# Expert weights in one transfer each, the last two bodies of an eight-image pipeline merged, and own weight sets and four banks for the last experts

## What is computed

```
x = x + deformable_conv(group_norm(x))             # F: 9 taps, gathered by learned offsets
x = x + top_ranks(sort(corr(group_norm(x))))       # S: every token's 1024 correlations sorted, 128 ranks kept
t = t + local_attention(layer_norm(t))             # C: windows 4, 16, 32
t = t + moe(layer_norm(t))                         # C: 8 experts 128 -> 128 -> 128, gelu, top 2 gates
t = t + state_space(layer_norm(t))                 # C: 8 heads, state 32
t = t + moe(layer_norm(t))                         # M: 8 experts, hidden 341, silu(h1) * h3, top 2 gates
```

## Time and profile before

| what | us |
|---|---|
| median of 3 runs | 5278.51 (5259.53 to 5298.2) |
| profiled execution | 5287.57 |
| its span, first to last instruction | 5285.8 |
| VectorE busy | 4563.2 (86%) |
| TensorE busy | 4040.3 (76%), mean granted clock 0.851 |
| ScalarE busy | 3051.8 (58%) |
| GpSimd busy | 927.3 (18%) |

### The profile page before, as it was taken

How to read it: one execution, slowest core, us unless ns; L and a number is a source line. 1 busy time by engine, 2 the same in 40 slices (tenths; PEclk the granted TensorE clock), 3 DMA queues, 4 the chain that set the end, 5 groups by cost and what they waited for, 6 DMA issues and landing times.

```text
span 5285.8 us, 59716 instructions
## 1 busy us (share of the span) xinstructions
PE 4040.3 (76%) x19026; PEld 2678.5 (51%) x19026; DVE 4563.2 (86%) x5779; ACT 3051.8 (58%) x7094; POOL 927.3 (18%) x580
## 2 busy tenths in 40 slices
PE   5665638988698868988698877988599876776487
PEld 4554325745366544755366444755357453443254
DVE  0298899999999999999999999999999999999721
ACT  4554226865487636866477646866377655653364
POOL 2253002600053002600044001610035000000000
PEclk8887568998799878998799888998799988886698
DMA  4232002310132012310032011310033000000011
GB/s 131 84 105 57 16 0 70 110 31 21 34 101 74 28 30 69 100 43 17 28 96 86 27 34 44 109 48 24 26 91 94 23 25 27 29 24 18 0 29 36
DMA packets 226078, 269.68 MB, mean 51 GB/s; under 512 B 26831, under 2 KB 188506, under 8 KB 225626
## 3 DMA queue, kind: packets, MB, share of 16 engines
q0 software_dynamic: 46080, 151.03, 9.8%
q1 hardware_dynamic: 179674, 114.65, 7.4%
HBM read 242.25 MB, written 23.34 MB: 50 GB/s over the span
## 4 chain that ended last, share of the span: by engine, by line
DVE 36%; PE 30%; issue 13%; ACT 8%; DMA 5%; POOL 4%; SPq 3%; DVEq 0%; POOLq 0%; ACTq 0%
PE bank L595 6%; POOL gath L733 4%; DVE srt_a L770 4%; DVE srt_b L770 3%; DMA gath<-quads,idx 3%; PE bank L1190 3%; DVE srt_a L813 2%; SPq L500 2%; DVE srt_b L813 2%; PE bank L1503 2%; PE bank L1507 2%; DVE srt_b L802 2%; DVE srt_a L802 2%; ACT diag L628 2%; DVE srt_a L768 2%
## 5 line engine op out<-in xcount | busy, mean ns | idle before, releaser
L733 POOL DMA_INDIRECT gath<-quads,idx x576 | 927.1, 1609 | 3137.6 <-DVE idx L704 2570.7
L595 PE MATMUL bank<-diag,gath 128*128 128x128 f32 x4608 | 619.0, 297 | 173.6 <-DMA gath<-quads,idx 173.6
L628 ACT ACTIVATE diag<-ident,w 128x128 f32<-128x128 f32 x2304 | 697.6, 391 | 12.8 <-DVE w L717 12.6
L595 PEld LDWEIGHTS bank<-diag,gath 128*128 128x128 f32 x4608 | 593.4, 211 | 205.1 <-DMA gath<-quads,idx 128.9
L1503 PE MATMUL bank<-mu_t,e2w 128*128 128x512 f32 (+1 forms) x768 | 453.2, 675 | 134.8 <-DMA e2w<-moe_w_t 117.9
L1487 PEld LDWEIGHTS bank<-e2w,act 128*128 128x128 f32 (+1 forms) x3072 | 423.9, 203 | 199.5 <-issue 175.7
L1507 PE MATMUL bank<-gated_u,e2w 128*128 128x512 f32 (+1 forms) x768 | 438.5, 655 | 31.9 <-ACT h_s L1561 31.9
L1487 PE MATMUL bank<-e2w,act 128*128 128x128 f32 (+1 forms) x3072 | 428.4, 286 | 18.9 <-DVE act L1591 18.9
L1591 DVE TENSOR_TENSOR act<-act,h_s 128x512 f32<-128x512 f32 (+1 forms) x384 | 262.6, 686 | 167.6 <-ACT h_s L1561 160.1
L1555 ACT ACTIVATE act<-bank 128x512 f32<-128x512 f32 (+1 forms) x384 | 228.7, 595 | 309.2 <-PE bank L1503 307.1
L811 DVE TENSOR_TENSOR srt_a<-srt_b 128x1920 f32<-128x1920 f32 (+5 forms) x176 | 381.0, 2165 | 3.7
(11 more groups left out here) (319 smaller groups left out, 7740.2 us busy)
## 6 DMA issues: line engine op xcount, KB each, us to landing
e2w<-moe_w_t SPq DMA_DIRECT2D x256, 170.5 KB
quads<-xn_tok SPq DMA_DIRECT2D x256, 64.0 KB
e1w<-L_ffn_w SPq DMA_DIRECT2D x256, 64.0 KB, 2.0
e2w<-moe_w_t SPq DMA_DIRECT2D x256, 64.0 KB
gath<-quads,idx POOLq DMA_INDIRECT x576
e2w<-moe_w_t SPq DMA_DIRECT2D x128, 42.5 KB
x_tok<-x SPq DMA_DIRECT2D x8, 512.0 KB, 4.0
out<-tm SPq DMA_DIRECT2D x16, 256.0 KB, 2.5
```

The source lines that it names most:

```text
L595: ins = T.matmul(FB[q % 2][:, k * P:(k + 1) * P], gath[:, g % 2, k, s * C:(s + 1) * C], diag[:, g % 2, 4 * k + s], start=(s == 0), stop=(s ...
L628: ins = SC.activation(diag[:, g % 2, n], ident[:], ACT.Copy, scale=w[:, n:n + 1])
L733: pool.indirect_dma_start(gath[:, g % 2, k], None, quads, bass.IndirectOffsetOnAxis(idx[:, TG * g + k:TG * g + k + 1], 0)).then_inc(sem["g ...
```

## The change

1. *Weights packed.* On the host w1, w3 and w2 of a second expert are laid side by side in one array of 128 rows by 1066 numbers (w2 padded with zeros from 341 to 384 rows), those of a first expert in 128 rows by 256. SP issues one transfer for each expert instead of five or two; the semaphore counts follow.
2. *Bodies 7 and 8 in one.* The late body now also holds C(7,1), M(7,0) and M(7,1); the drain body and its strings are gone. The order within a stream stays.
3. *Last second experts, M(7,1).* Each of the eight experts has its own place, three in `srt_a`, three in `srt_b`, two in `corr`, and its own semaphore; SP issues the eight loads once half 1 of image 7 is ranked. Its h1, h3 and gated inputs go round four banks (FB[0], FB[1], MB[0], MB[1]) instead of two.
4. *New strings* for the full and late bodies on TensorE, ScalarE, SP and VectorE. Those of fill and early are as they were.

```diff
-    SP_full=(
-        "CCCMMFFCCCCCCCCMMMFMMMCCCCMMMCMMMMMMM"
+    SP_full=(
+        "CCCMMFFCCCCMCCCCMMMMMMMMFCCCCMCMMMMMM"
...
-    SP_late=(
-        "CCCMMMCCCMCCCCCMMMMMMMMMMMMMCCMCCC"
+    SP_late=(
+        "CCCMMMCCCMCCCCCMMMMMMMMMMMMMCCCMMMCCCCCMMMMCMCCCMCMMMMMMMMMM"
...
-                sp.dma_start(e1w[:, e % E1_SLOTS, 0], A["L2_ffn_w1"][e]).then_inc(sem["e1_in%d" % (e % E1_SLOTS)], 16)
-                sp.dma_start(e1w[:, e % E1_SLOTS, 1], A["L2_ffn_w2"][e]).then_inc(sem["e1_in%d" % (e % E1_SLOTS)], 16)
+                sp.dma_start(e1w[:, e % E1_SLOTS].rearrange("p a c -> p (a c)"), A["moe1_w_t"][e]).then_inc(sem["e1_in%d" % (e % E1_SLOTS)], 16)
...
+        def last_unit(i, h):
+            return isinstance(i, int) and i == IMGS - 1 and h == 1
+
+        def experts_w(i, h, e):
+            if not last_unit(i, h):
+                return e2w[:, e % 2]
+            size = 2 * HID + 3 * C
+            home = (srt_a, srt_b, corr)[e // 3][:].rearrange("p g n -> p (g n)")
+            return home[:, e % 3 * size:(e % 3 + 1) * size]
+
+        def wide_banks(i, h):
+            return (FB[0], FB[1], MB[0], MB[1]) if last_unit(i, h) else (MB[0], MB[1])
+
         def sp_M(sp, i, h):
             for e in range(E8):
-                sp.wait_ge(sem["y2_ps"], unit("y2_ps", i, h, max(0, 3 * (e - 1))))
+                if last_unit(i, h):
+                    sp.wait_ge(sem["ranked"], unit("ranked", i, h))
+                else:
+                    sp.wait_ge(sem["y2_ps"], unit("y2_ps", i, h, max(0, 3 * (e - 1))))
                 settle(sp)
-                sp.dma_start(e2w[:, e % 2, 0:HID], A["moe2_w1_t"][e]).then_inc(sem["e2_in%d" % (e % 2)], 16)
-                sp.dma_start(e2w[:, e % 2, W3:W3 + HID], A["moe2_w3_t"][e]).then_inc(sem["e2_in%d" % (e % 2)], 16)
-                for k, m in enumerate(HTILES):
-                    sp.dma_start(e2w[0:m, e % 2, W2 + k * C:W2 + (k + 1) * C],
-                                 A["moe2_w2_t"][e, k * P:k * P + m]).then_inc(sem["e2_in%d" % (e % 2)], 16)
+                arrived = last_in[e] if last_unit(i, h) else sem["e2_in%d" % (e % 2)]
+                sp.dma_start(experts_w(i, h, e), A["moe2_w_t"][e]).then_inc(arrived, 16)
                 yield
...
+            X = wide_banks(i, h)
             pe.wait_ge(sem["m_utsb"], unit("m_utsb", i, h))
+            if last_unit(i, h):
+                pe.wait_ge(sem["corr_sb"], img("corr_sb", i))
...
-                    if r >= 2:
-                        pe.wait_ge(sem["m_sb"], unit("m_sb", i, h, r - 1))
-                    T.matmul(MB[r % 2][0:m, :], e2w[:, e % 2, k * P:k * P + m], mu_t[:], start=True, stop=True).then_inc(sem["m_ps"], 1)
+                    if r >= len(X):
+                        pe.wait_ge(sem["m_sb"], unit("m_sb", i, h, r - len(X) + 1))
+                    T.matmul(X[r % len(X)][0:m, :], experts_w(i, h, e)[:, k * P:k * P + m], mu_t[:], start=True, stop=True).then_inc(sem["m_ps"], 1)
...
             body(IMGS - 1, False, True, True)
-            body(IMGS, False, False, True)
-
-        def second_of(make, eng, i, sort, second):
-
-            if second and sort:
+
+        def second_of(make, eng, i, first, sort, second):
+
+            if second and not first:
+                return both(make(eng, i - 1, 1), make(eng, i, 0), make(eng, i, 1))
+            if second:
                 return both(make(eng, i - 1, 1), make(eng, i, 0))
...
+        def experts_of(make, eng, i, first, second):
+
+            if not second:
+                return both()
+            if first:
+                return both(make(eng, i - 1, 0), make(eng, i - 1, 1))
+            return both(make(eng, i - 1, 0), make(eng, i - 1, 1), make(eng, i, 0), make(eng, i, 1))
```

The string of VectorE for the late body, before (its last 96 letters of 382; the drain body's 108 follow) and after (its last 202 of 490):

```diff
-        "SSSCSCSSCSSSSSSSSSSCSCSSCSSCCCCSSCSSCCSSSCSSSCCSSSCCSSSSSCCSSSSCSSCSSCSSSSSSSSSSSSSSSSSSSSSSSS"
+        "SSCSCSCSSSSSSSSSSCSCSSCSCCCCSCSSCSCSSSSCSSSCCSSSSCCSSSCCSSSSSCSSCSSCSMSMSSSMMMMMMSSSSMSMMSMSMSMS"
+        "SSSMSMSMSSSSMSMSSCMCCCMCCMMCCCCCCCCMCMCCMCCMMCMCCMCCMMCCCCCCCCCCCCCCCCCCCCMMMMMMMMMMMMMMMMMMMMMM"
+        "MMMMMMMMMM"
```

More of the change, by code:

```diff
@@ L120 @@
[L120 to L129, removed]
@@ L331, in build @@
         prep = ctx.enter_context(nc.semaphore("prep"))
+        last_in = [ctx.enter_context(nc.semaphore(f"last_in{e}")) for e in range(E8)]
         n_loads = [0]
@@ L1487, in y_part @@
                     ins = T.matmul(MB[2][:, t * P:(t + 1) * P], act2[0:m, n % ACT2_SLOTS, t * P:(t + 1) * P],
-                                   e2w[0:m, e % 2, W2 + k * C:W2 + (k + 1) * C], start=False,
+                                   experts_w(i, h, e)[0:m, W2 + k * C:W2 + (k + 1) * C], start=False,
                                    stop=(n == 3 * E8 - 1 and t == UT - 1))
@@ L1554, in act_M @@
                     act.wait_ge(sem["y2_ps"], unit("y2_ps", i, h, n - ACT2_SLOTS + 1))
-                SC.activation(act2[0:m, n % ACT2_SLOTS], MB[r % 2][0:m, :], ACT.Silu).then_inc(sem["m_sb"], 1)
+                SC.activation(act2[0:m, n % ACT2_SLOTS], X[r % len(X)][0:m, :], ACT.Silu).then_inc(sem["m_sb"], 1)
                 yield
@@ L1620, in run @@
             body(IMGS - 1, False, True, True)
-            body(IMGS, False, False, True)
-        def second_of(make, eng, i, sort, second):
-            if second and sort:
+        def second_of(make, eng, i, first, sort, second):
+            if second and not first:
+                return both(make(eng, i - 1, 1), make(eng, i, 0), make(eng, i, 1))
+            if second:
                 return both(make(eng, i - 1, 1), make(eng, i, 0))
-            if second:
-                return make(eng, i - 1, 1)
             if sort:
@@ L1631, in second_of @@
             return both()
-        def experts_of(make, eng, i, second):
-            return both(make(eng, i - 1, 0), make(eng, i - 1, 1)) if second else both()
+        def experts_of(make, eng, i, first, second):
[4 more added lines that the diff above has]
+            return both(make(eng, i - 1, 0), make(eng, i - 1, 1), make(eng, i, 0), make(eng, i, 1))
         block = ctx.enter_context(nc.Block())
@@ L1646, in body @@
                 weave(sp, "SP", kind_of(first, sort, second),
-                      dict(F=sp_first(sp, i, first, more), C=second_of(sp_C, sp, i, sort, second), M=experts_of(sp_M, sp, i, second)))
+                      dict(F=sp_first(sp, i, first, more), C=second_of(sp_C, sp, i, first, sort, second), M=experts_of(sp_M, sp, i, first, second)))
             def sp_first(sp, i, first, more):
@@ L1672, in body @@
                 weave(act, "ACT", kind_of(first, sort, second),
-                      dict(F=act_F(act, i, sort, first), C=second_of(act_C, act, i, sort, second), M=experts_of(act_M, act, i, second)))
+                      dict(F=act_F(act, i, sort, first), C=second_of(act_C, act, i, first, sort, second), M=experts_of(act_M, act, i, first, second)))
             run(act, body)
@@ L1684, in body @@
                            S=both(dve_S(dve, i, 0), dve_S(dve, i, 1)) if sort else both(),
-                           C=second_of(dve_C, dve, i, sort, second), M=experts_of(dve_M, dve, i, second)))
+                           C=second_of(dve_C, dve, i, first, sort, second), M=experts_of(dve_M, dve, i, first, second)))
             run(dve, body)
@@ L1705, in body @@
                 weave(pe, "PE", kind_of(first, sort, second),
-                      dict(F=pe_F(pe, i, sort, first), C=second_of(pe_C, pe, i, sort, second), M=experts_of(pe_M, pe, i, second)))
+                      dict(F=pe_F(pe, i, sort, first), C=second_of(pe_C, pe, i, first, sort, second), M=experts_of(pe_M, pe, i, first, second)))
             run(pe, body)
@@ L1743, in layouts @@
         w_out_t=t(a["L3_attn_W_out"].T.reshape(2, P, C).transpose(1, 0, 2)),
-        moe2_w1_t=t(a["L3_ffn_w1"].transpose(0, 2, 1)), moe2_w3_t=t(a["L3_ffn_w3"].transpose(0, 2, 1)),
-        moe2_w2_t=t(a["L3_ffn_w2"].transpose(0, 2, 1)),
+        moe1_w_t=t(np.concatenate([a["L2_ffn_w1"], a["L2_ffn_w2"]], 2)), moe2_w_t=t(packed),
   )
```

94 lines of the change are left out of this document (49 added, 45 removed).

## The result

The changed kernel takes 5344.4 us, median of 4 runs (5332.92 to 5358.25), against 5278.7 us of the kernel before in the same session. The ratio is 1.0124 with a 95% interval from 1.0101 to 1.0147: slower by 1.2%. The forecast was 5229 us, its range 5185 to 5272; both the sign and the range are missed.

A forecast was written before the change was run, and what follows sets the result against it. VectorE, busy 86% of the span, was taken to bound all but the end. Terms 13 - 21 - 35 - 6 = -49 gave 5238.6 us for the profiled execution, 5229 us from the median; range 5185 to 5272.

The forecast's parts named there:

- New strings for full bodies, 0: Six full bodies: VectorE's work is equal, so only waits change; 0 us, at most -174 if all waits went.
- Rival C: Full bodies: second experts' products not ready stop VectorE's sort, 1.2 us at each of 16, +118 to 5347 us; chance 0.12.
- M(7,0) ahead of the sort, +13: Late body: M(7,0) work moved before the sort's end makes the sort end 13 us later; bounds +10 and +22.
- C(7,1), -21: Last half image's attention, first experts and state space, with less M(7,0) beside them: 200.5 to 180 us; bounds -45 and +5.
- state-space term, 94 to 84: State-space part of C(7,1): 15 us of other work leaves the chain, 5 added for lower clock, 94 to 84 us.
- rival B: C(7,1) is bound by its own chain at the lower clock and stays at 200 us; 5250 us in all; chance 0.12.
- Own sets, -35: M(7,1): with own weight places six late experts take 8.46 us instead of 14.14; -35 us, bounds -28 and -40.
- Rival D: Moved loads or wide banks don't work, M(7,1) stays at 14.14 us an expert; 5263 us; chance 0.05.
- Four banks, 0: M(7,1): TensorE had no gap with two banks, so two more bring 0 us; bounds 0 and -4.
- one transfer per expert, -6: Weight loads: latency stays, only SP's issue time falls; 1 us per body, -6 us in six; bounds -20 to +10.
- Rival A: C(7,1) follows TensorE's work, -45 instead of -21, and full bodies lose 2 us of waits each; 5193 us; chance 0.24.

The follow-up runs named there:

- experiment 6: The kernel before with one packed transfer for each expert, first and second, and nothing else: 5272.91 us, ratio 0.9981.
- (7): Two runs from experiment 1: shared weight slots instead of own sets for M(7,1), 5274.15 us; two banks instead of four there, 5242.06 us.
- (8): experiment 1 with the last two bodies separate again, on the old late and drain strings; own weight sets and four banks stay: 5245.48 us, ratio 0.9929.
- experiment 1: The changed kernel with the full bodies' four strings of the kernel before, everything else of the change kept: 5247.52 us, ratio 0.9931.
- experiment 2: The kernel before with the four new strings for the full bodies and nothing else of the change: 5389.11 us, ratio 1.019.
- Experiment 4: The changed kernel with four first-expert weight slots instead of three and the fourth load ahead of the 32 transfers in SP's full string: 5281.0 us, ratio 0.9992.
- i1: experiment 1 with only the two banks MB[0] and MB[1] for M(7,1) instead of four, own weight sets kept: 5242.06 us, ratio 0.9933.

## Why the prediction was wrong

Measured parts, against the kernel before: packing -10 (experiment 6), own sets -27 (7), merge about 0 (8), banks 0 (7), full strings +97 (marks; experiment 1 gives 5344.4 - 5247.5 = 97 too, and experiment 2, in the kernel before, +107 by its marks). The sum is +60, and 5278.7 + 60 = 5339 us beside 5344.4 measured. Without the strings the parts are -37, where the forecast had -49, and experiment 1's 5247.5 us lies inside the stated range: the rest of the forecast held within 12 us.

**New strings for full bodies, 0: this step failed, and it alone turned the sign.** It measured +97 us. I had looked at how far second experts and first experts move against the sort, and not at F. With the new strings the group norm is done 8 us later and the 32 transfers start 10 us later, and SP holds the fourth load of the first experts behind them: VectorE's waits at the first experts grew by 75 us in six bodies. The strings also raised its waits at the second experts, by 28. Experiment 4 took the first cause away and left 49 us. The rows were there: the earlier trace rows was only the largest wait, while the 2.98 us of TensorE for that load, shown above, told that the load had no slack. "VectorE's work is equal, so only waits change" was right; that these would come out at zero had no row behind it. The reading of the strings was off too: VectorE's second experts stand earlier by up to 40 sort steps, not 36, and its last four steps of F by up to 17 later, which the prediction did not look at.

**Rival C had sign and size (5347), mostly by the wrong waiter.** It put 1.2 us on each of 16 second experts, 118 us in six bodies. Shown instead are 75 us at the first experts, most of it one wait of 11.6 us a body for the fourth load; C's own mechanism is worth 28, under 5 us a body. That the total met the measured time within 3 us is luck. Its point of decision, 8.2 us more waits a body, was passed: they were 16.

**M(7,0) ahead of the sort, +13.** Right: the late body is 590.3 us against 574.1 for the same load without the merge, +16. Experiment 1 showed +22, the upper bound, and i1 with the same strings +15.

**C(7,1), -21.** Right in kind and a third to a half too large. From the sort's end to M(7,1)'s statistics 200.5 us became 185.1, or 189.2 in experiment 1, so -15 and -11. The start wait of 8.7 us went as forecast. The state-space term, 94 to 84, did not come: 91 to 95 us remain. That is rival B for this part, at granted 0.80 in the kernel after and 0.73 in experiment 1, where I had put 5 us on a lower clock. The whole exchange of late body and C(7,1) is then about zero, where I had -8.

**Own sets, -35.** M(7,1) fell from 122.5 us in steps: to 118.3 by packing, to 114.9 in the merged body, to 88.2 by the sets (-27), and 86.8 in the kernel after. The term is at, or 1 us past, its bound of -28. A step is 8.82 us, not 8.46. It wasn't the clock, as the window of one expert after shows beside the earlier trace rows (columns as above):

```profile
5306.89:5315.71 8.82, 8.82 (x47) 5.67 (x46) 2.07 (x3) 5.32 (x11) 0.00 (x0) 1.00 0.00 0
```

TensorE is busy throughout at 1.00 in both, but the window of the earlier trace rows holds 45 matmuls and this one 47. What I had taken for an expert began with a product that had waited less (1.43 against 1.91 us in the earlier trace rows) in the first expert of the half, and the steps come to their pace only after it: from 5271.63 to 5324.52 us of the kernel after there are six of 8.82. So I took a length from the start of a series. The loads were hidden, as forecast. Rival D (14.14 us an expert) falls.

**Four banks, 0, and one transfer per expert, -6.** The first is right; only the first step of the half is shorter with four (7.91 us in experiment 1, 8.46 in i1). The second measured -10 (-20 to -1), of the right kind: latency stays (3.7 us to landing, against 3.8 from the first of five issues to the matmul), SP's time falls. But the full bodies gained nothing, so my 1 us a body was at the wrong place.

**Rival A** failed on both its parts, though for C(7,1) TensorE was indeed nearly full before: with less to do it ran at a lower granted clock and the part took as long.

**What stays open:** which letters of ScalarE's and TensorE's strings delay the group norm, and which make the products of the second experts late. The second is worth 28 us in the kernel after and 48 once the queue is out of the way. No run changed it.

## What to carry to other kernels

A queue of transfer issues is an engine in order like any other: where a load needed just in time shares it with a block of bulk transfers, compute when that block starts and ends, and what moves it, before any string of the order is changed. Put such a load ahead of the block and give it a buffer to land in. And when a wait has been removed, count the others again: of 70 us taken away at one place here, 20 came back at the next. And when work is taken out from beside a dependent chain, ask what the chain does on its own: here it took the same time at a lower clock.

## What the runs showed of the hardware

- 32 transfers to `quads` held SP for 22.5 us, 0.70 us each on average. A packed weight load cost it 0.44 to 0.54 us in the blocks of three and two above and 0.33 alone (in experiment 4, at 2699.06), as much as a plain one. The Trainium skill, "DMA: Bandwidth & Descriptors", section "Issuing engines are not separate DMA queues", says the time a sequencer needs to start a DMA is usually small beside the DMA. For one transfer the trace agrees (0.5 against 3.7 us); for a block of 32 in front of a load that is waited for it was not small: moving the load ahead of the block, with a slot for it, took 48 us off the full bodies.
- A packed load of 533 KB lands 3.7 us after its issue, about as fast as five pieces (3.8 to the matmul). Three, three and two in a row land after 4.7, 7.2 and 9.1 us, medians of the profile after:

```profile
srt_a<-moe_w_t SPq DMA_DIRECT2D x3, 533.0 KB, 4.7
srt_b<-moe_w_t SPq DMA_DIRECT2D x3, 533.0 KB, 7.2
corr<-moe_w_t SPq DMA_DIRECT2D x2, 533.0 KB, 9.1
```

- The state space with TensorE 63 of 92 us busy ran at a granted clock of 0.80; with 81 of 96 us at 0.91. With TensorE full, in M(7,1)'s experts, the clock was 1.00 with two banks before and with four after.
- Behind the 11.05 us in which it stood, TensorE's next 6.2 us ran at the lower level (granted 0.50, columns as above), and its pair of matmuls took 2.07 us; behind the 2.98 us of before the same pair took 1.12, at 0.95 granted over the first 2 us, and only then came 6 us at 0.50.

```profile
2703.00:2709.20 6.20, 6.16 (x13) 2.94 (x14) 1.98 (x2) 0.69 (x1) 0.00 (x0) 0.50 0.00 0
```
